# Fused attention, sparse branch and gated MLP: the 64 selected rows of x fetched by an indirect transfer in place of one-hot products

## What is computed

```python
gate = (x @ W_ig).transpose(0, 2, 1)                 # 8 gate heads, 1024 tokens
_, top_idx = jax.lax.top_k(gate, 8)                  # 8 tokens for each head: 64 rows
sel = take_along_axis(x @ W_ip, top_idx)             # per head, 128 wide
sq, sk, sv = sel @ W_sq, sel @ W_sk, sel @ W_sv
so = softmax(sq @ sk.T / sqrt(128)) @ sv             # 8 x 8 for each head
io = (so @ W_io).mean(over the 8 tokens)             # one row for each head
attn = attn + io                                     # added to the main attention's heads
```

## Time and profile before

| | |
|---|---|
| median of 3 runs | 682.4 us (680.27 to 683.05) |
| the profiled execution | 682.62 us |
| its span, first to last instruction | 680.8 us |
| mean granted TensorE clock | 0.991 |
| busy: PE, DVE, ACT, POOL | 642.5, 474.5, 400.2, 371.5 us |
| transfers | 49.85 MB; those of SP in queue q1 (22144 packets), those of ACT in queue q10 (1376); none issued by POOL |

### The profile page before, as it was taken

One profiled execution on the slowest core, in us unless ns is written; L12 is line 12 of the kernel. 1 busy time (PEld: TensorE's weight loads), 2 busy tenths in 40 slices (PEclk: granted clock), 3 DMA queues, 4 the chain that ended last, 5 costly groups with the idle time before them and its releaser, 6 DMA issues.

```text
span 680.8 us, 14087 instructions
## 1 busy us (share of the span) xinstructions
PE 642.5 (94%) x4456; PEld 582.8 (86%) x4456; DVE 474.5 (70%) x1291; ACT 400.2 (59%) x934; POOL 371.5 (55%) x331
## 2 busy tenths in 40 slices
PE   7989999999999999999999999999999999889895
PEld 5878988899889988998889888988899888779895
DVE  3886467666766667666856586658666768997996
ACT  4775246744774485656564757456754767545552
POOL 6874278464744484456628472737454725521564
PEclk8989999999999999999999999999999999989999
DMA  7306232510461037103610343114510482000001
GB/s 224 126 2 148 70 69 63 125 57 1 110 147 54 0 92 162 54 0 92 140 53 23 92 94 67 54 46 93 115 54 0 112 239 74 10 1 1 1 17 47
DMA packets 23551, 49.85 MB, mean 73 GB/s; under 512 B 3168, under 2 KB 16352, under 8 KB 21600
## 3 DMA queue, kind: packets, MB, share of 16 engines
q1 hardware_dynamic: 22144, 47.82, 27.5%
q10 hardware_dynamic: 1376, 1.64, 0.7%
HBM read 16.94 MB, written 1.05 MB: 26 GB/s over the span
## 4 chain that ended last, share of the span: by engine, by line
PE 57%; DVE 14%; ACT 13%; issue 10%; POOL 4%; DMA 1%; ACTq 0%; DVEq 0%; POOLq 0%; SPq 0%
PE J L840 5%; PE J L842 4%; PE J L841 4%; PE J L873 4%; ACT Pb L1165 4%; PE J L889 3%; PE J L886 3%; ACT kvraw L1260 3%; PE J L885 3%; DVE SC L1375 3%; DVE PTl L1306 3%; PE SC L860 3%; PE SC L863 3%; PE SC L861 3%; PE SC L864 3%
## 5 line engine op out<-in xcount | busy, mean ns | idle before, releaser
L1306 DVE TENSOR_TENSOR PTl<-J,PTh 128x512 fp32r<-128x512 f32 (+1 forms) x192 | 102.8, 553 | 66.7 <-ACT PTh L1148 65.7
L1165 ACT ACTIVATE Pb<-SC,nm 128x128 f32<-128x128 f32 (+7 forms) x128 | 94.9, 742 | 56.6 <-DVE nm L1375 56.4
L1375 DVE CUSTOM_DVE_ANT_0 SC<-SC,mask 128x128 f32<-128x128 f32 (+7 forms) x128 | 97.1, 758 | 20.7 <-PE SC L864 19.6
L873 PE MATMUL J<-ident,Pb 128*128 128x128 f32 x576 | 88.0, 278 | 9.1 <-ACT Pb L1165 7.6
L1148 ACT ACTIVATE PTh<-J 128x512 fp32r<-128x512 f32 (+1 forms) x192 | 88.1, 492 | 7.2 <-PE J L873 6.6
L873 PEld LDWEIGHTS J<-ident,Pb 128*128 128x128 f32 x576 | 63.7, 141 | 19.1 <-ACT Pb L1165 8.9
L885 PE MATMUL J<-PTh,Vh 128*128 128x256 f32 x320 | 76.0, 273 | 0.8 <-DVE PTl L1306 0.8
L886 PE MATMUL J<-PTh,Vl 128*128 128x256 f32 x320 | 74.5, 280 | 0.0
L860 PE MATMUL SC<-KNh,QNh 128*128 128x128 f32 (+2 forms) x192 | 69.4, 361 | 0.1
L863 PE MATMUL SC<-KK,QS 128*128 128x128 f32 (+2 forms) x192 | 66.1, 344 | 0.0
L861 PE MATMUL SC<-KNl,QNh 128*128 128x128 f32 (+2 forms) x192 | 66.1, 344 | 0.0
(11 more groups left out here) (305 smaller groups left out, 1914.3 us busy)
## 6 DMA issues: line engine op xcount, KB each, us to landing
KK<-RK SPq DMA_DIRECT2D x30, 512.0 KB, 6.3
QS<-RQh SPq DMA_DIRECT2D x15, 256.0 KB, 7.5
QS<-RQl SPq DMA_DIRECT2D x15, 256.0 KB, 6.5
KX<-KX SPq DMA_DIRECT2D x14, 256.0 KB, 2.3
QX<-QX SPq DMA_DIRECT2D x14, 256.0 KB, 2.4
r_kv<-in_W_ckv SPq DMA_DIRECT2D x7, 384.0 KB, 3.6
r_o<-in_W_o SPq DMA_DIRECT2D x18, 128.0 KB, 2.1
r_qn<-in_W_qT SPq DMA_DIRECT2D x16, 128.0 KB, 2.1
```

What stands on the lines that cost most here:

```text
L873: last = pe.transpose(o[:, tile(j - 4 * c)], Pb[i % 2][:, tile(j)], ident[:, :])
L1165: act.activation(Pb[i % 2][:, w], SC[i % 2][:, s], ACT.Exp, bias=nm[:, i % 2:i % 2 + 1], scale=-1.0, accum_out=sm[:, b, i:i + 1]).then_inc ...
L1306: dve.tensor_tensor(o, i, h.bitcast(F32), ALU.subtract).then_inc(done[kind], 1)
L1375: dve.tensor_tensor_reduce(out=SC[i % 2][:, s], in0=SC[i % 2][:, s], in1=mask[:, 128 * (7 - i):S], scale=-SCALE, scalar=HIGH, op0=ALU.add, ...
```

## The change

The one-hot table and its products go. `side` 2 now puts the 64 indices in a column, one on each of 64 partitions; DVE casts them to integers in `selidx`; POOL issues an indirect transfer from x in device memory that brings row `selidx[p]` to partition p of `selrow` (64 x 256, 64 KB). `side` 3 and 4 are one PE transpose each of half of `selrow`. `side` 2 is moved ahead of the scores of tile 6, and `side` 3 and 4 behind the output projection of head 0. The wait of the first accumulation for `side` 4 goes, and so does the load of `tokid`.

```diff
-        tokid = sb("tokid", [128, T])
+        selidx = sb("selidx", [64, 1], U32)
-        oneh = QX[:, 0, 512:1024].rearrange("p (t n) -> p t n", t=T)
-        idxb = QX[:, 1, 0:64]
+        selrow = QX[0:64, 0, 512:768]
...
-            ("qk", 0, 5), ("pv", 0, 1), ("exp", 0, 5), ("top8", 0, 3), *t(0, 4), ("kt", 1, 1),
-            ("qk", 0, 6), ("side", 0, 2), ("exp", 0, 6), *t(0, 5), ("wosp", 2, 0), ("wqn", 2, 0), ("wqp", 1, 0), ("kv", 1, 0),
-            ("side", 0, 3), ("side", 0, 4), ("wo", 0, 0), ("wo", 0, 1),
+            ("qk", 0, 5), ("pv", 0, 1), ("exp", 0, 5), ("top8", 0, 3), *t(0, 4), ("kt", 1, 1), ("side", 0, 2),
+            ("qk", 0, 6), ("exp", 0, 6), *t(0, 5), ("wosp", 2, 0), ("wqn", 2, 0), ("wqp", 1, 0), ("kv", 1, 0),
+            ("wo", 0, 0), ("wo", 0, 1), ("side", 0, 3), ("side", 0, 4),
...
-            for dst, src in ((blk[:, :], c_blk), (tokid[:, :], c_tok), (off64[:, :], c_off), (mean8[:, :], c_mean)):
+            for dst, src in ((blk[:, :], c_blk), (off64[:, :], c_off), (mean8[:, :], c_mean)):
...
+                    if kind == "side" and c == 2:
+                        gp.wait_ge(side_dve, 5)
+                        gp.wait_ge(rq_ready, 1)
+                        gp.indirect_dma_start(selrow, None, x[:, :], bass.IndirectOffsetOnAxis(selidx[:, 0:1], 0)).then_inc(ld_sel, 16)
...
                 if c == 2:
                     pe.wait_ge(side_dve, 4)
-                    return mm(o[:, 0:64], lhsT=ones8, rhs=i8d[:, :], start=True, stop=True)
+                    return mm(o[0:64, 0:1], lhsT=i8d[:, :], rhs=ones8[:, 0:1], start=True, stop=True)
                 if c in (3, 4):
-                    pe.wait_ge(side_dve, 5)
-                    pe.wait_ge(ld_x, 16)
-                    for t in range(T):
-                        last = mm(o[:, 0:64], lhsT=acc[:, t, tile(c - 3)], rhs=oneh[:, t, :], start=t == 0, stop=t == T - 1)
-                    return last
+                    pe.wait_ge(ld_sel, 16)
+                    return pe.transpose(o[:, 0:64], selrow[:, tile(c - 3)], ident[0:64, 0:64])
...
                 if c == 2:
-                    cp(idxb, o[:, 0:64]).then_inc(d, 1)
+                    cp(selidx[:, :], o[0:64, 0:1]).then_inc(d, 1)
                     dve.wait_ge(d, 3)
-                    a = idxb.rearrange("p (a n) -> p a n", a=1).to_broadcast([128, T, 64])
-                    bb = tokid[:, :].rearrange("p (t a) -> p t a", a=1).to_broadcast([128, T, 64])
-                    dve.tensor_tensor(oneh[:, :, :], a, bb, ALU.is_equal).then_inc(side_dve, 1)
+                    dve.sem_inc(side_dve, 1)
...
-                        if isinstance(u, int) and u == 0 and c == 0:
-                            dve.wait_ge(ready["side"], 5)
```

More of the change, by code:

```diff
@@ L58, in attention_and_mlp @@
                       W_ip, W_sq, W_sk, W_sv, W_io, W_upT, W_gateT, W_downT,
-                      c_ident, c_cs, c_tok, c_blk, c_off, c_mean, out):
+                      c_ident, c_cs, c_blk, c_off, c_mean, out):
     top = ExitStack()
@@ L221, in attention_and_mlp @@
         soT = sb("soT", [128, 8])
-        ld_x, ld_vec, ld_w0, ld_side, ld_wip = sem("ld_x"), sem("ld_vec"), sem("ld_w0"), sem("ld_side"), sem("ld_wip")
+        ld_x, ld_vec, ld_w0, ld_side, ld_wip, ld_sel = (sem("ld_x"), sem("ld_vec"), sem("ld_w0"), sem("ld_side"), sem("ld_wip"),
+                                                       sem("ld_sel"))
         ld_xt = [sem(f"ld_xt{c}") for c in range(4)]
@@ L638, in _ @@
             sp.wait_ge(stored, 80)
-        LD_SIDE, LD_W0, LD_WS = 16 * 4, 16 * 3, 16 * 4
+        LD_SIDE, LD_W0, LD_WS = 16 * 3, 16 * 3, 16 * 4
         def rope(eng, X, hi_, lo_, swapped, mul, rdy, u):
@@ L1601, in constants @@
                           np.tile(np.stack([-sin, sin], axis=-1).reshape(S, ROPE).T, (2, 1))], axis=1),
-        "c_tok": (np.arange(128)[:, None] + 128 * np.arange(T)[None, :]).astype(np.float32),
         "c_blk": (np.arange(8)[:, None] == col[None, :] // TOPK).astype(np.float32),
```

## The result

| | before | changed |
|---|---|---|
| median | 682.7 us | 691.3 us (688.98 to 693.52, 4 runs) |
| ratio of the two, 95% interval | | 1.013 (1.0097 to 1.0163) |
| the profiled execution | 682.62 | 693.52 |
| its span | 680.8 | 691.7 |
| mean granted TensorE clock | 0.991 | 0.976 |

The change makes the kernel 1.3% slower. I had said 680.4, with a range up to 684.6: wrong in size and in sign.

A forecast was written before the change was run, and what follows sets the result against it. PE was taken as the bound. Terms -3.56 - 0.24 + 0.45 + 0.8 + 0.3 + 0.25 gave -2.0 us, so a median of 680.4 us from 682.4, with a range of 679.1 to 684.6.

The forecast's parts named there:

- Does the gather land by 65.7?: Indirect load before PE's transposes: index written at 61.5, transfer 3.6 us, descriptors 0.6, landing 65.7, no stall.
- Behind the backlog: Rival: engines first finish SP's transfers, gather lands at 72.5, PE stands 6.8 us, +4.8, about 688 us; chance 0.11.
- the price of the clock: Rival: close PE waits lower the granted clock, losing 1.6 us of work, 682.0 us; shares 0.15 with a little late.
- c2 ahead of the scores: Index product before tile 6's scores: PE stalls 1.5 us at 57 for the index table, 0.45 us left as cost.
- DVE: Index-column copy ahead of tile 6's score operation moves it from 61.12 to 61.4; the dropped comparison pays nothing.
- The PSUM bank: Before the output projection's second half, PE stands 0.8 us until DVE frees the bank of tile 5's first transposes.
- The products that go, and the turn behind the gather: PE saves 3.56 us of one-hot products and 0.24 idle; two transposes cost 0.3, a wait before W_ip 0.25.
- POOL and SP: POOL has 11 us of slack, so nothing queued behind the gather is late; SP's dropped 4 KB load counts nothing.
- Index by index: Rival: POOL handles 64 indices singly, 11.6 us (+7.2, 690 us) or 5.4 by the skill (+1.0); chance 0.06.
- Shift held as a block: Later stretches start from PE products, so they should move together with the shift, give or take 0.7 us.
- A little late: Rival: descriptors 2.91 and transfer 3.6 us, landing 68.1, PE stands 2.4, +0.4, 682.8 us; shares 0.15 with the clock.

The follow-up runs named there:

- e3: Changed kernel with a plain GpSimd load of the first 64 rows of x in place of the indirect transfer; 687.05 us, one execution.
- e4: Changed kernel with the plain load of the first 64 rows of x issued by ACT in its own queue instead of POOL; 689.59 us, one execution.
- e2: Changed kernel, but SP issues the K and Q stack copies for head 1 only once the gather has landed; 680.34 us, ratio 0.9961 to the kernel before.
- e7: e2 with the index product c2 back in its old place behind the scores of tile 6; 679.58 us, ratio 0.9948 to the kernel before.
- e1: Changed kernel plus 25 unused 512-column products keeping PE busy before its wait for the gather; 687.24 us, ratio 1.0074 to the kernel before.
- e6: Kernel before, with only the index product c2 moved ahead of the scores of tile 6; 685.18 us, ratio 1.0032 to the kernel before.
- e8: Changed kernel timed again without any edit; 688.42 us, ratio 1.0073 to the kernel before.
- e5: Changed kernel with the gather's use moved behind tile 7's scores, a kv product and a P times V; 682.43 us, ratio 0.999 to the kernel before.
- e10: Changed kernel with the stack copies left ahead of the gather and the W_ip load held until it has landed; 684.21 us, one execution.
- e9: e7 with tile 7's scores between the output projection's halves and the first W_ip products later; 680.5 us, ratio 0.9966 to the kernel before.

## Why the prediction was wrong

**The step that failed: "Does the gather land by 65.7?"** It landed at 71.70. I had the end of the range, 72.5 by r_o, and put it aside with the sentence that what made r_o late was the traffic ahead of it in its own queue. e3 and e4 show that the queue is not what counts. The rival "Behind the backlog", to which I gave 0.11, is what happened. It could have been priced by bytes. From 55.5 on SP had issued W_sq to W_io, W_ip, the stacks, r_o and, just then, r_qn: 256 + 1024 + 1536 + 256 KB, 3.1 MB. At the 130 GB/s of the window from 56 to 60 and the 264 of that from 60 to 66, some 1.0 MB had moved by the gather's issue at 61.8. The 2.1 MB left, at the 222 GB/s that the trace of before shows from 66 to 70, are an estimate of 9.5 us, to 71.3. The last packet of SP's started at 71.7; the gather's own moved at 69.6 to 70.5, and it landed at 71.70.

The Trainium skill (*DMA: Bandwidth & Descriptors*, "Queues, rings and completion order") says that each engine takes turns between queues that have work. Here no gain from it over the backlog can be seen: 64 KB in a queue of its own, POOL's or ACT's, landed 9.4 to 10.9 us after issue behind SP's traffic, and its packets mingled only with SP's last ones. The same page's 2.0 us plus the bytes (its section on the anatomy of one DMA), an estimate of 2.15, is near to the 2.7 of e2 and e7, where the engines were almost free; it is no price for a full one.

**The second miss, the price of the clock.** I gave 1.6 us, read off a dip of 4 us, and only among the rivals: the sum has no term for it. In the profiled executions of the changed kernel it was about 9, since the low clock lasted for 23.9 us. Without the clock the "backlog" rival would have been near: -2.0 and a wait of 5.62 make +3.6, and the shift of e1 is 3.6.

**c2 ahead of the scores.** Wait 1.31 (1.5 predicted), kv product at 61.66 against 61.7. The stall itself was right, but in e6 the place costs about 2 us in the median, 0.45 by my sum; between e2 and e7 it is 0.8 and not clear of noise. What the sum leaves out is again the clock: it fell after the wait of 1.3 in the profiles of e2 and e6, and not in those of the changed kernel (both, with e8), e1, e3, e4, e5 and e10.

**DVE.** Its scores of tile 6 came at 61.70 for a predicted 61.4; the whole profile was 0.2 late there.

**The PSUM bank.** 1.23 against 0.8, with the second half at 65.26 for 64.95: right in kind, 0.3 to 0.4 short, as DVE's PTl began at 64.51 and not at 64.2. e7 has 1.02.

**The products that go, and the turn behind the gather.** In e7 the transposes are at 65.63 and the scores of tile 7 at 65.89, 2.3 us early, as the mark is. So the terms -3.56, -0.24, +0.8, +0.3 and +0.25 stand together, -2.45, once the gather is in time and c2 is in its old place.

**POOL and SP.** The split of W_o was at 72.18 (72.57 before): nothing queued behind the gather was late, as forecast. Index by index is refuted with both of its prices, 11.6 and 5.4 us: 64 indices cost POOL 1.15 us in all.

**Shift held as a block.** Right, nearly: 13.2 in head 1, 12.45 at 602 us, 0.75 less where I had allowed 0.7. (In "A little late" the landing adds up to 68.0, not 68.1; nothing hangs on it.)

**Still open.** What sets how long the low clock lasts: 23.9 us in two profiles and 6.8 in two others after waits of 5.0 to 5.6 us, 10.2 in e10 after one of 2.24, 6.8 in e9 after shorter ones, 3.4 in e2 and e6 after 1.3. Also whether the engines take work strictly by the time of issue: the packets of the changed kernel fit it, but shown is only that 64 KB in POOL's and in ACT's queue moved when W_ip and nearly all of the stacks had gone.

## What to carry to other kernels

In this kernel a small transfer that PE waited for took as long as the DMA engines needed for what they still had to move when it was issued, whether it stood in POOL's queue or in ACT's. So before you add one, add up the bytes issued and not landed, divide by the rate in the windows, and compare with the moment of use. If it is too late, hold back the large transfers that nobody needs yet (one wait on SP took the changed kernel, at a median of 688.4 in e8 and 691.3 before that, down to 680.3), or use the result later. Price a long wait of PE with the clock that falls in it, and look at the windows behind the wait for how long it stays low.

## What the runs showed of the hardware that I had not expected

- The granted clock stayed at 0.50 for 20 us in which PE was busy throughout (8.00 of 8.00 us in two windows), after one wait of 5.0 to 5.6 us. In e3 and e4 it came back 6.8 us after it fell.
- 25 products of 512 columns that nobody uses, 5.34 us in PE's timeline, put where PE would have waited as long, kept it at 1.00 (e1).
- It also fell after much shorter waits, in some profiles only: to 0.50 for 10.2 us after 2.24 us (e10), for 3.4 us after 1.3 us (e2 and e6, not the changed kernel).
- An indirect transfer of 64 rows of 1 KB costs POOL 1.15 us and lands in 2.7 to 2.8 with the engines nearly free; a plain one of the same size costs POOL 0.77.
- With W_ip and the stacks, 2.6 MB, issued ahead by SP, 64 KB took 9.4 to 10.9 us in POOL's queue and 10.0 in ACT's.
